# Expert blocks of 128 rows in place of 256, and a plain float32 first layer, in a mixture-of-experts stage

## The reference

```
xt = m.reshape(-1, Dd)                                # 1024 rows of 256
probs = jax.nn.softmax(xt @ Wg, axis=-1)              # 8 experts
wts, idx = jax.lax.top_k(probs, K)                    # K = 2
wts = wts / jnp.sum(wts, axis=-1, keepdims=True)
h1 = jax.nn.gelu(jnp.einsum('td,edf->etf', xt, W1) + b1[:, None, :])   # W1: 8 x 256 x 1024
ye = jnp.einsum('etf,efd->etd', h1, W2) + b2[:, None, :]               # W2: 8 x 1024 x 256
sel = ye[idx, jnp.arange(T)[:, None], :]
moe_out = jnp.sum(wts[..., None] * sel, axis=1).reshape(Bb, Ss, Dd)
```

## Time and profile before

| | |
|---|---|
| median of 3 runs | 1062.91 us (1062.78 to 1072.04) |
| span of the profiled execution | 1060.4 us |
| PE busy | 1019.5 us, 96% of the span |
| DVE, ACT, POOL busy | 647.4 us, 469.6 us, 243.5 us |
| expert blocks, first hidden matmul to last output matmul | from 533.6 us to 718.3 us in the trace |
| moved by DMA | 72.54 MB |

### The profile page before, as it was taken

The page is one execution under the profiler, slowest core; times in us unless marked ns, Lnnn a source line. Parts: engine busy times, 40 slices in busy tenths (PEclk is TensorE's granted clock), DMA queues, the critical chain, the costliest instruction groups (busy, mean ns, idle before and its releaser), DMA issues.

```text
span 1060.4 us, 27662 instructions
## 1 busy us (share of the span) xinstructions
PE 1019.5 (96%) x11767; PEld 879.2 (83%) x11767; DVE 647.4 (61%) x1399; ACT 469.6 (44%) x863; POOL 243.5 (23%) x381
## 2 busy tenths in 40 slices
PE   5999999999999999999899999997999999999998
PEld 5888888888888787887689999996888888887887
DVE  5645645545333555776869999986667663355242
ACT  3333333333333556543156677762534433464232
POOL 2311211211111133442414444422211100011000
PEclk9999999999999999999889999999999999999999
DMA  9400000000000630220136557612111002000000
GB/s 306 140 2 21 21 2 21 2 1 1 2 1 2 227 123 3 81 101 13 43 79 239 198 199 257 239 61 90 41 38 47 12 2 72 3 2 2 1 20 20
DMA packets 55401, 72.54 MB, mean 68 GB/s; under 512 B 8488, under 2 KB 48624, under 8 KB 54640
## 3 DMA queue, kind: packets, MB, share of 16 engines
q1 hardware_dynamic: 53744, 66.59, 18.8%
q0 software_dynamic: 1536, 4.20, 1.3%
HBM read 59.76 MB, written 11.01 MB: 67 GB/s over the span
## 4 chain that ended last, share of the span: by engine, by line
PE 87%; DVE 7%; ACT 3%; issue 2%; DMA 1%; POOL 0%; DVEq 0%; ACTq 0%; POOLq 0%
PE ps L624 9%; PE ps L639 9%; PE ps L2321 8%; PE ps L2337 7%; PE ps L2684 5%; PE ps L1512 4%; PE ps L608 3%; PE ps L656 3%; PE ps L1430 3%; PE ps L1146 3%; PE ps L578 3%; PE ps L676 2%; PE ps L1469 2%; PE ps L1529 2%; PE ps L1081 2%; PE ps L1071 2%
## 5 line engine op out<-in xcount | busy, mean ns | idle before, releaser
L379 POOL TENSOR_TENSOR rn_tmp<-rn_cur,eps 128x1 f32<-128x1 f32 x48 | 14.1, 294 | 358.9 <-DVE rn_cur L373 358.7
L767 ACT ACTIVATE x0pT<-ps 128x512 f32<-128x512 f32 x64 | 38.3, 598 | 123.6 <-PE ps L639 123.6
L2321 PE MATMUL ps<-moe_xT_hi,ew_1hi 128*128 128x256 f32 x240 | 69.9, 291 | 2.3 <-DVE moe_xT_lo L2471 2.3
L2337 PE MATMUL ps<-ew_2hi,eh_hi 128*128 128x256 f32 x240 | 69.3, 289 | 2.5 <-DVE eh_lo L2479 2.5
L2321 PE MATMUL ps<-moe_xT_lo,ew_1hi 128*128 128x256 f32 x240 | 69.0, 288 | 0.0
L2321 PE MATMUL ps<-moe_xT_hi,ew_1lo 128*128 128x256 f32 x240 | 69.0, 287 | 0.0
L2477 DVE CAST eh_hi<-eh 128x512 fp32r<-128x512 f32 x60 | 61.1, 1018 | 11.0 <-ACT eh L2383 10.9
L2337 PE MATMUL ps<-ew_2hi,eh_lo 128*128 128x256 f32 x240 | 67.0, 279 | 0.0
L2337 PE MATMUL ps<-ew_2lo,eh_hi 128*128 128x256 f32 x240 | 66.9, 279 | 0.0
L876 DVE TENSOR_TENSOR x0A_lo<-ps,x0A_hi 128x512 fp32r<-128x512 f32 x64 | 41.1, 685 | 31.7 <-ACT x0A_hi L758 31.7
L2684 PE MATMUL ps<-f,ffw 128*128 128x512 f32 x256 | 59.1, 391 | 0.8 <-issue 0.6
(11 more groups left out here) (340 smaller groups left out, 2846.2 us busy)
## 6 DMA issues: line engine op xcount, KB each, us to landing
ew<-L_ffn_W_dram SPq DMA_DIRECT2D x30, 1024.0 KB, 7.2
x0cin<-ctx_dram SPq DMA_DIRECT2D x8, 512.0 KB, 4.2
x1cin<-ctx_dram SPq DMA_DIRECT2D x8, 512.0 KB, 4.0
moe_out<-moe_y SPq DMA_DIRECT2D x15, 256.0 KB, 7.8
xg<-moe_in SPq DMA_DIRECT2D x14, 256.0 KB, 7.8
moe_in<-padneg SPq DMA_DIRECT2D x3, 1024.0 KB, 12.4
maskrow<-mask_BxS_ik_dram SPq DMA_DIRECT2D x2, 1024.0 KB, 8.2
x0wk<-L_xattn_Wkv_dram SPq DMA_DIRECT2D x1, 1024.0 KB, 7.7
```

Source lines behind the costliest of these rows:

```text
L767: nc.scalar.activation(g.pT[:, u, :], ps[:, S_BANK[u % 2], :], ACT.Exp, scale=64.0 ** -0.5).then_inc(C0.exp, 1)
L2321: last = nc.tensor.matmul(ps[:, n % 3, j * BT:j * BT + BT], w[b % 2][:, i, f * P:f * P + P], v[b % 2][:, i, :], start=(i == 0 and m == 0), ...
L2337: last = nc.tensor.matmul(ps[:, O_BANK[b % 2] + c, 0:D], v[n % 3][:, j * BT + c * P:j * BT + c * P + P], w[b % 2][:, f, :], start=(f == 0 ...
```

## The change

Blocks have 128 rows, so that there are 2 x 1024 / 128 + 8 - 1 = 23 of them, 15 of which have an owner known at run time. The first layer is computed in plain float32, one matmul for a product, and neither W1 nor the rows are split any more. The second layer stays in split products. `n` now counts half blocks (`NP` = 2, with `NF` = 4 slices in each). The four raw weight buffers (`NW` = 4) are loaded early for blocks 0 to 3; W1 and W2 have semaphores of their own. There are three buffers of upper parts of W2; its lower parts overwrite the raw values in place. Rows (`NG`) and results (`NY`) have four buffers each. POOL has no part in the block loop any more: DVE makes all lower parts, two pieces in a block. The norm's weights are applied to the rows on DVE. The one-hot matrices place the rows of two blocks (`PLACED`).

```diff
 XVW = 18
 E, F = 8, 1024
 FT = F // P
-BT = 256
+BT = 128
+PLACED = 2
+NW, NY, NG = 4, 4, 4
 NB = 2 * B * N // BT + E - 1
...
-        ew1, ew2, ew1_hi, ew2_hi, ew1_lo, ew2_lo = ([sb(f"ew{i}{n}", shape, dt) for i in range(2)] for n, shape, dt in (
-            ("_1", [P, KD, F], F32), ("_2", [P, FT, D], F32), ("_1hi", [P, KD, F], F32R), ("_2hi", [P, FT, D], F32R),
-            ("_1lo", [P, KD, F], F32R), ("_2lo", [P, FT, D], F32R)))
+        ew1 = [sb(f"ew{i}_1", [P, KD, F]) for i in range(NW)]
+        ew2_at = at[0]
+        ew2 = [sb(f"ew{i}_2", [P, FT, D]) for i in range(NW)]
+        ew2_lo = [nc.alloc_sbuf_tensor_at(f"ew{i}_2lo", [P, FT, D], F32R, offset=ew2_at + 4 * FT * D * i) for i in range(NW)]
+        ew2_hi_at = at[0]
+        ew2_hi = [sb(f"ew{i}_2hi", [P, FT, D], F32R) for i in range(3)]
         yg = [nc.alloc_sbuf_tensor_at(f"yg{i}", [P, 2, D], F32, offset=yg_at + 8 * D * i) for i in range(4)]
...
+
 
         def expert_upper(act, b, i):
-            hi, lo, w = expert_part(b, i)
-            act.wait_ge(ld_e[b % 2], 32 * (b // 2) + 32)
-            if b > 1:
-                act.wait_ge(MO.h_ps if i < 2 else MO.o_ps, NP * (b - 1))
-            nc.scalar.activation(hi, w, ACT.Copy).then_inc(MO.w_hi, 1)
+            sl = slice(NF * i, NF * i + NF)
+            act.wait_ge(ld_w2[b % NW], 16 * (b // NW) + 16)
+            if b == 2:
+                act.wait_ge(MO.b1x, 1)
+            if b > 2:
+                act.wait_ge(MO.o_ps, NP * (b - 2))
+            nc.scalar.activation(ew2_hi[b % 3][:, sl, :], ew2[b % NW][:, sl, :], ACT.Copy).then_inc(MO.w_hi, 1)
 
         def expert_lower(dve, b, i):
-            hi, lo, w = expert_part(b, i)
-            dve.wait_ge(MO.w_hi, 4 * b + i + 1)
-            nc.vector.tensor_tensor(lo, w, hi.bitcast(F32), ALU.subtract).then_inc(MO.w_lo_dve, 1)
-
-        def expert_lower_pool(pool, b, i):
-            hi, lo, w = expert_part(b, i)
-            pool.wait_ge(MO.w_hi, 4 * b + i + 1)
-            nc.gpsimd.tensor_tensor(lo, w, hi.bitcast(F32), ALU.subtract).then_inc(MO.w_lo_pool, 1)
+            sl = slice(NF * i, NF * i + NF)
...
 
             def hidden(n):
                 b, p = divmod(n, NP)
                 if p == 0:
-                    pe.wait_ge(MO.xT_lo, b + 1)
-                    pe.wait_ge(MO.w_lo_dve, 2 * b + 1)
-                    pe.wait_ge(MO.w_lo_pool, 2 * b + 1)
+                    pe.wait_ge(MO.xT, b + 1)
+                    pe.wait_ge(ld_w1[b % NW], 16 * (b // NW) + 16)
                 if n > 2:
                     pe.wait_ge(MO.gelu, n - 2)
-                for j in range(2):
-                    f = 2 * p + j
+                for j in range(NF):
+                    f = NF * p + j
                     for i in range(KD):
-                        for m, (w, v) in enumerate(((ew1_hi, xT_hi), (ew1_hi, xT_lo), (ew1_lo, xT_hi))):
-                            last = nc.tensor.matmul(ps[:, n % 3, j * BT:j * BT + BT], w[b % 2][:, i, f * P:f * P + P], v[b % 2][:, i, :],
-                                                    start=(i == 0 and m == 0), stop=(i == KD - 1 and m == 2))
+                        last = nc.tensor.matmul(ps[:, n % 3, j * BT:j * BT + BT], ew1[b % NW][:, i, f * P:f * P + P], xT[b % 2][:, i, :],
+                                                start=(i == 0), stop=(i == KD - 1))
                 last.then_inc(MO.h_ps, 1)
 
             def outputs(n):
                 b, p = divmod(n, NP)
                 pe.wait_ge(MO.split, n + 1)
-                if p == 0:
-                    pe.wait_ge(MO.w_lo_dve, 2 * b + 2)
-                    pe.wait_ge(MO.w_lo_pool, 2 * b + 2)
-                    if b > 1:
-                        pe.wait_ge(MO.y_sb, b - 1)
-                for j in range(2):
-                    f = 2 * p + j
-                    for c in range(2):
-                        for m, (v, w) in enumerate(((eh_hi, ew2_hi), (eh_hi, ew2_lo), (eh_lo, ew2_hi))):
-                            last = nc.tensor.matmul(ps[:, O_BANK[b % 2] + c, 0:D], v[n % 3][:, j * BT + c * P:j * BT + c * P + P], w[b % 2][:, f, :],
-                                                    start=(f == 0 and m == 0), stop=(f == FT - 1 and m == 2))
+                pe.wait_ge(MO.w_lo, n + 1)
+                if p == 0 and b > 3:
+                    pe.wait_ge(MO.y_sb, b - 3)
+                for j in range(NF):
+                    f = NF * p + j
+                    for m, (v, w) in enumerate(((eh_hi[n % 3], ew2_hi[b % 3]), (eh_hi[n % 3], ew2_lo[b % NW]), (eh_lo[n % 3], ew2_hi[b % 3]))):
+                        last = nc.tensor.matmul(ps[:, o_bank(b), 0:D], v[:, j * BT:j * BT + BT], w[:, f, :],
+                                                start=(f == 0 and m == 0), stop=(f == FT - 1 and m == 2))
                 last.then_inc(MO.o_ps, 1)
 
             hidden(0)
             hidden(1)
             for n in range(NP * NB):
+                b, p = divmod(n, NP)
                 if n + 2 < NP * NB:
                     hidden(n + 2)
-                if n % NP == 0 and n // NP + 1 < NB:
-                    rows_T(n // NP + 1)
+                if p == 0 and b + 2 < NB:
+                    rows_T(b + 2)
                 outputs(n)
...
+
             hidden(0)
             hidden(1)
             for n in range(NP * NB):
                 b, p = divmod(n, NP)
                 if n + 2 < NP * NB:
                     hidden(n + 2)
-                if p == 0 and b + 1 < NB:
-                    rows_T(b + 1)
-                if p < 2 and 0 < b < NB - 1:
-                    expert_upper(act, b + 1, 2 + p)
-                if p == 1 and b > 0:
+                if b + 2 < NB:
+                    expert_upper(act, b + 2, p)
+                if p == 0 and b > 0:
                     result(b - 1)
-                if p >= 2 and b + 2 < NB:
-                    expert_upper(act, b + 2, p - 2)
                 if n == NP * (NB - 1):
                     x1_weights_upper(act)
...
+            def rows_T(b):
+                dve.wait_ge(MO.xT_ps, max(b, 1))
+                if b > 1:
+                    dve.wait_ge(MO.h_ps, NP * (b - 1))
+                for k in range(KD):
+                    src = ps[:, XT_BANK, k * BT:k * BT + BT] if b >= PLACED else ps[:, FIRST_BANK + k, b * BT:b * BT + BT]
+                    last = nc.vector.tensor_scalar(xT[b % 2][:, k, :], src, vec("ln2_g", k), vec("ln2_b", k), ALU.mult, ALU.add)
+                last.then_inc(MO.xT, 1)
+
...
                 if n + 2 < NP * NB:
                     hidden(n + 2)
-                if p == 0 and b + 1 < NB:
-                    rows_T(b + 1)
-                if n == 1:
-                    owners_biases()
-                if p == 0 and 0 < b < NB - 1:
-                    expert_lower(dve, b + 1, 2)
-                if p == 2 and b + 2 < NB:
-                    expert_lower(dve, b + 2, 0)
+                if p == 0 and b + 2 < NB:
+                    rows_T(b + 2)
+                if b + 2 < NB:
+                    expert_lower(dve, b + 2, p)
                 if n == NP * (NB - 1) + 1:
...
-                sp.wait_ge(MO.w_lo_dve, 2 * (b - 2) + 2)
-                sp.wait_ge(MO.w_lo_pool, 2 * (b - 2) + 2)
+                sp.wait_ge(MO.h_ps, NP * (b - NW + 1))
+                sp.wait_ge(MO.o_ps, NP * (b - NW + 1))
                 if b < E:
                     expert(b, slice(b, b + 1))
                 else:
@@ -2811,31 +2776,33 @@
                     e = sp.value_load(owner_i[0:1, b - E:b - E + 1], min_val=0, max_val=E - 1)
                     expert(b, bass.ds(e, 1))
 
-            weights_of(2)
-            weights_of(3)
+            def store_of(b):
+                sp.wait_ge(MO.y_sb, b + 1)
+                sp.dma_start(block_rows(moe_out, b), ysb[b % NY][:, :]).then_inc(y_stored[b % NY], 16)
+
             sp.wait_ge(MO.spread, 16 * 2 * T)
-            rows_of(1)
-            rows_of(2)
+            for b in range(PLACED, PLACED + NG):
+                rows_of(b)
             for b in range(NB):
-                if b < 2:
-                    sp.wait_ge(MO.pad, b)
-                    if b == 0:
+                if b in (0, 4):
+                    i = b // 4
+                    if i > 0:
+                        sp.wait_ge(MO.pad, i)
+                    if i == 0:
                         for i in range(2):
                             sp.dma_start(maskTi[:, :, i], a["mask_BxS2_ik0"].rearrange("b (k p) -> k p b", k=2)[i],
                                          allow_slow_non_contiguous=True).then_inc(ld["pad"], 16)
-                    whole(maskrow[:, :, :], a["mask_BxS2_ik0"].rearrange("(o h b) s -> h o b s", o=1, h=2)[b].broadcast_to((P, B // 2, S)), ld["pad"])
-                if b + 3 < NB:
-                    rows_of(b + 3)
+                    whole(maskrow[:, :, :], a["mask_BxS2_ik0"].rearrange("(o h b) s -> h o b s", o=1, h=2)[b // 4].broadcast_to((P, B // 2, S)), ld["pad"])
                 if b > 0:
-                    sp.wait_ge(MO.y_sb, b)
```

(57 more changed lines are left out.)

115 lines of the change are left out of this document (52 added, 63 removed).

## The result

The changed kernel takes 1115.0 us (median of 4 runs, 1106.45 to 1117.41) against 1063.09 of before in the same measurement: 1.0461 times as long, 95% interval [1.0407, 1.0516], that is 52 us slower. The forecast was 1101 with a range of 1080 to 1118. A timed run lies 1.8 us above its span (1116.7 against 1114.9), not 2.5. Ratios leave out runs more than 1.5% above the fastest of the same kernel; here that is one run, of the kernel that loads W2 ahead of W1. Lines of the code are shifted: the first layer is L2311, the second L2324, W1 and W2 are loaded at L2714 and L2715, the upper parts are L2255, the result's copy L2368, its store L2781.

The account below looks back on a forecast made before the run. Waiting for one load at a time, not PE, was to bound the block loop: load 4 at 552, plus 185.7 us of turns, plus the end, 756.5, 38 us later. 1060.4 + 38 = 1098.6 span, 1101 median, range 1080 to 1118.

Parts of the forecast that it names:

- The ring: Block loop: a load is issued only after the last one landed, through ACT and SP; turn 9.6 or 10.3 us.
- masks and tiles: Second mask and two context tiles queued in the block loop: about 0.8 us each, bringing 183.3 us to 185.7.
- SP's terms: SP in each turn: 0.09 us from release to issue, 0.45 for the store, 0.70 for reading the owner's number.
- the landing: Block loop, each load: from W1's issue until W2 has landed, taken as 7.7 us, from 7.4 to 8.2.
- the rival with a short fixed part: Block loop: a transfer's fixed part is short, turns of 8.7 and 9.4 us, 1084 us; chance 0.04.
- When load 4 is issued: Start of the expert blocks: first load inside the loop issued at 552 us at the 1.2 GHz clock, 550 at 2.4.
- The end: After the last load: load 22 issued at 737.7, W2 there at 745.4, last output matmul 11 us later, 756.5.
- PE's block: PE's work for one new block: 16 first-layer matmuls, 24 second-layer, 2 transposes, 4.9 us; 113 us for 23 blocks.
- PE stays the bound: Rival, block loop: PE sets the pace at 23 x 4.9 us, total 1002 us; chance 0.02.
- several loads are under way: Rival, block loop: loads overlap, DMA alone sets 6.2 us a block, total 1035 us; chance 0.08.
- What lies beside: Other engines: POOL leaves the loop, DVE 5.0 and ACT 4.5 us a block, worth nothing; attention at most 1 us gained.
- The break-even turn: Rival, block loop: a shorter landing gives turns of 8.1 us on average, time within 1% of before; chance 0.02.

Follow-up runs that it names:

- the second run: The changed kernel as it is, with no edit, measured once more: 1107.1 us, 1.040 of before.

## Why the prediction was right, and where it wasn't

**The ring.** Right, in its place, its order and its members. Undone at either of two places it gives the time back (49 to 57 and 65 to 73 us); each member that was changed alone (owner's number, W2's landing) moved the turn; and every load of the loop had its wait on ACT. The turn was 10.70 us for a forecast of 10.3, and 10.26 without the number for 9.7 (9.6, and 2.4 us of masks and tiles over 18 turns). SP's terms were good: 0.44 us from store to W1, 1.15 with the number in most turns, for 0.45 and 1.15; and from the start of the upper part to the store 1.36 for 1.43. The term that was mis-sized is the landing: 7.7 us from W1's issue (7.8 with the masks and tiles), which I had lowered from 8.0 because the rows and the store behind it are only half as large now. In the turn shown it was 624.62 - 616.25 = 8.4. From W1's issue to the start of the upper part it is 8.27 on average over the 18 turns (7.9 to 9.3), just beyond the 7.4 to 8.2 that the prediction allowed; none came near the 6.8 of the rival with a short fixed part. The row of before with its 8.0 was the better guide than my correction of it. Cost: 192.6 - 185.7 = 7 us.

**When load 4 is issued.** 552 forecast, 562.5 in the profiled run, 551.5 in the second one. The step was the clock: it was taken as low from 538 on, not from 500, because the profile of before has the low clock only from 522 on the earlier trace rows. It wasn't known from one profile that this point moves. Its size is 10.5 us, the largest single error. Part of the hit in the second run is luck: hidden(4) was priced at 1.8 us, as 8 matmuls at 0.22, but it is 16 rows, which at the low clock are 3.5 us; they took 2.06 in the profiled run, because the clock was up again (1.00 from 550 to 560).

**The end.** From load 22's issue to the last output matmul 772.3 - 755.1 = 17.2 us, forecast 18.8. So 10.5 + 6.9 - 1.6 = 15.8 us, of the 16.3 by which the span (1114.9 for 1098.6) was missed.

**PE's block.** Wrong, and it was luck that the forecast did not suffer. The prediction multiplied 16 matmuls of the program by the price of one of the 16 rows in a chain link; but the program issues 8 matmuls at L1413, so each has two rows, and 128 columns cost 224 ns. The page of the changed kernel has 736 rows for the first layer's 23 x 16 = 368 matmuls (busy, 101.5 us, is far less than 736 x 297 ns: the rows overlap, and their mean length is not their price):

```profile
L2311 PE MATMUL ps<-moe_xT,ew 128*128 128x128 f32 x736 | 101.5, 297 | 39.4 <-issue 29.7
```

A block takes PE 32 x 0.112 + 24 x 0.119 + 0.2 = 6.6 us, not 4.9, and what PE alone gives back is 15 x 11.88 - 23 x 6.64 = 25 us, not 60. With the weights ahead of the store the whole kernel gained 23. The ring hid the error at the full clock only. For the low clock the prediction says that PE's block, 42 x 0.22 = 9.2 us, is still below the ring; with the rows counted right it is 58 x 0.22 = 12.8 us, above the ring's 10.3. At the clock near 0.5 that it expected, PE and not the ring would have set the pace by its own prices. The clock was wrong too, 0.93 in the loop, and the two errors cancelled. The rival "PE stays the bound" at 1002 could not have happened at any speed of DMA; "several loads are under way", put at 1035 by DMA's rate, came to 1042 with PE as the limit.

**What lies beside.** I expected PE busy about half the time at a clock near 0.5; it was 73% at 0.93. PE's larger block leaves shorter gaps, and the clock mostly stayed up; whether the one made the other was not tried. The break-even turn of 8.1 us fits: a turn of 8.5 measured 0.8% over before.

## What to carry to other kernels

More buffers don't put more loads in flight if a load's issue stands behind a store, whose data stands on an in-order engine behind a wait for the load before: walk each queue around once, from a load's issue to the next one's, and where the walk returns to a landing, the pace is the round trip (10.7 us here) and not the rate (6.2). Before costing a deeper pipeline, set weights that are free to go ahead of whatever only passes by; here the order of two calls was worth 65 to 73 us.
And count an instruction's rows against the program's calls before taking a price from a row: in this profile a plain float32 matmul is two rows, which turned a price of 224 ns into 112.

## What the runs showed of the hardware

In a row without gaps, at the full clock, a float32r matmul with 128 moving columns took 110 ns and one with 256 took 118 to 119; plain float32 took 224 and 432 ns, in two rows each. Of two transfers of 1 MB that SP issued back to back, the second was there 8.3 us after the first's issue on average, and the first, in the kernel that loads W2 first, 6.1 us after its own. The granted clock fell at about 500 us in some executions of the changed kernel and after 522 in others, at a cost of some 10 us; what decides it stays open.
